# A vision-tower layer on one core: limits exchanged a step earlier, output weights split in two places, factors and residual biases moved into attention steps

## The reference

```python
def reference(x, ...):
    h = s4d_kernel(...)                      # (16, 128, 1024): 16 tiles of 128 tokens, 1024 features
    h = h + attn(layernorm(h), Wq, bq, Wk, bk, Wv, bv, Wo, bo)
    h = h + ffn(layernorm(h), gate, up, down)
    return h

def attn(x, ...):                            # 32 heads of 32 features
    q, k, v = (x @ W.T + b, split into heads)
    scores = where(causal, q @ k.T / sqrt(32), -inf)
    return (softmax(scores) @ v) @ Wo.T + bo

def qlinear(x, q, scale, A, Bm):             # gate, up: 1024 -> 2752, down: 2752 -> 1024
    w = (q - 7.5) * (scale * 0.005)
    return x @ w.T + 0.02 * (x @ A @ Bm)     # A, Bm of rank 32
# ffn(x) = qlinear_down(silu(qlinear_gate(x)) * qlinear_up(x))
```

## Time and profile before

| what | value |
|---|---|
| median of 3 runs | 2070.15 us (2068.34 to 2071.24) |
| the profiled execution: its time, its span | 2068.1 us, 2066.1 us |
| busy in the span: PE, DVE, ACT, POOL | 1894.4, 1166.4, 614.9, 614.3 us |
| attention steps 24 to 31 | 721.3 to 884.4 us of the span |
| output stage | 884.4 to about 1105 us |
| feed-forward stage | about 1105 us to the end |

### The profile page before, as it was taken

How to read it: one execution, slowest core, us unless ns; L and a number is a source line. 1 busy time by engine, 2 the same in 40 slices (tenths; PEclk the granted TensorE clock), 3 DMA queues, 4 the chain that set the end, 5 groups by cost and what they waited for, 6 DMA issues and landing times.

```text
span 2066.1 us, 31321 instructions
## 1 busy us (share of the span) xinstructions
PE 1894.4 (92%) x13212; PEld 1027.5 (50%) x13212; DVE 1166.4 (56%) x1476; ACT 614.9 (30%) x871; POOL 614.3 (30%) x261
## 2 busy tenths in 40 slices
PE   0377699999999988989999999999999999999999
PEld 0377565666666655544554444444444444444444
DVE  8999568777788777755564544444444444211111
ACT  2155333433443334421113333333333233200000
POOL 2675023343343333434211232222223222111101
PEclk9998799999999999999999999999999999999999
DMA  2022212111112111234433232232232132533441
GB/s 90 10 72 61 55 32 55 39 40 36 49 54 66 67 47 52 71 134 150 168 122 98 83 102 79 75 102 90 64 102 92 62 102 78 192 132 109 141 143 42
DMA packets 99812, 173.32 MB, mean 84 GB/s; under 512 B 13984, under 2 KB 75168, under 8 KB 91744
## 3 DMA queue, kind: packets, MB, share of 16 engines
q1 hardware_dynamic: 99680, 171.41, 26.0%
HBM read 114.22 MB, written 56.11 MB: 82 GB/s over the span
## 4 chain that ended last, share of the span: by engine, by line
PE 76%; DVE 6%; POOL 2%; issue 1%; ACT 1%; DMA 1%; SPq 0%; ACTq 0%; DVEq 0%; POOLq 0%
PE acc L1133 15%; PE acc L1207 14%; PE acc L1134 14%; PE ps_p L937 4%; PE ps_p L939 4%; PE ps_p L938 4%; PE ps_t L964 2%; PE acc L1051 2%; PE ps_p L953 2%; PE ps_p L955 2%; PE ps_p L954 2%; PE acc L1052 2%; PE acc L1053 2%; PE ps_l L1149 2%; PE ps_i L1163 1%
## 5 line engine op out<-in xcount | busy, mean ns | idle before, releaser
L1133 PE MATMUL acc<-x_hi,q_f 128*128 128x512 f16 x1376 | 522.0, 379 | 0.0
L1134 PE MATMUL acc<-x_lo,q_f 128*128 128x512 f16 x1376 | 521.5, 379 | 0.0
L1207 PE MATMUL acc<-down_levels,hid_parts 128*128 128x512 f16 x1376 | 300.1, 379 | 0.0
L897 POOL TENSOR_TENSOR prob<-prob,mx 128x1024 f32<-128x1024 f32 x64 | 121.5, 1898 | 405.0 <-DVE mx L1489 405.0
L1133 PEld LDWEIGHTS acc<-x_hi,q_f 128*128 128x128 f16 x1376 | 134.5, 98 | 174.8 <-issue 17.8
L1207 PEld LDWEIGHTS acc<-down_levels,hid_parts 128*128 128x128 f16 x1376 | 133.2, 98 | 163.1 <-issue 5.0
L1134 PEld LDWEIGHTS acc<-x_lo,q_f 128*128 128x128 f16 x1376 | 134.7, 98 | 156.9
L906 POOL TENSOR_SCALAR q_f<-q_raw 128x2048 f16<-128x2048 int32 x22 | 118.1, 5366 | 312.6 <-PE acc L1134 311.8
L937 PE MATMUL ps_p<-x_hi,w_qk 128*128 128x512 f16 x512 | 197.2, 385 | 0.0
L939 PE MATMUL ps_p<-x_hi,w_qk 128*128 128x512 f16 x512 | 196.3, 383 | 0.0
L938 PE MATMUL ps_p<-x_lo,w_qk 128*128 128x512 f16 x512 | 196.3, 383 | 0.0
(11 more groups left out here) (285 smaller groups left out, 3087.1 us busy)
## 6 DMA issues: line engine op xcount, KB each, us to landing
q_raw<-in_gu_q SPq DMA_DIRECT2D x22, 1024.0 KB, 7.2
...
w_raw<-in_w_qk SPq DMA_DIRECT2D x8, 1024.0 KB, 5.2
...
wv_raw<-in_w_o SPq DMA_DIRECT2D x8, 1024.0 KB, 4.9
```

The lines of the kernel that those rows point to most:

```text
L897: nc.gpsimd.tensor_tensor(prob[s % 2][p][:], prob[s % 2][p][:], bc(mx[p][:], H, 2), ALU.subtract).then_inc(s_sub[p], 1)
L1133: nc.tensor.matmul(acc[u % 2][:, m, :], lev, x2_hi[:, k, tok], start=(k == 0), stop=False)
L1134: last = nc.tensor.matmul(acc[u % 2][:, m, :], lev, x2_lo[:, k, tok], start=False, stop=(k == KT - 1))
L1207: last = nc.tensor.matmul(acc[n % 2][:, b, :], parts[n % 3][:, at], levels[:, i, b * CH:(b + 1) * CH], start=(i == 0 and part == 0), stop= ...
```

## The change

- SP exchanges the limits at the head of step 23 instead of its end, and then loads gu_a_raw at once instead of in step 30.
- `WO_STEP` goes from 26 to 25, and the two blocks of Wo of a step are split: the first stands on ACT and DVE before and behind the second part of the probabilities (a = 1), the second before the values. `factors` moves to step 24 of DVE, the Sqrt that feeds it to the head of step 24 of ACT, gu_a's high half to step 25 of ACT and its low half to step 26 of DVE.
- POOL adds the bias to the first two residuals inside the last attention step: one before its subtractions, one between them and its multiplications.
- SP loads the attention output n + 3 before it stores h1 n.

Computation and instruction counts stay the same.

```diff
--- before.py
+++ after.py
@@ -562,7 +562,7 @@
 
 STAT_STEPS = (16, 17, 18, 19, 21, 22)
 LIMIT_STEP = 23
-WO_STEP = 26
+WO_STEP = 25
 
 
 def layer(nc, t, out, first, rooms, small, xn_hi, xn_lo, ident, mask, h0_dram):
@@ -771,6 +771,9 @@
                 sp.wait_ge(s_proj, place(V_STEPS - 1, 2) + 1)
                 for n in range(3):
                     load_output(n)
+            if s == LIMIT_STEP:
+                exchange_limits()
+                sp.dma_start(araw[:], t["gu_a"]).then_inc(s_araw, 16)
             if s >= 2:
                 store(s - 2)
             if c == 0 and j + 1 < KT:
@@ -783,15 +786,12 @@
                 first.exchange(sp, 2 + s // 10)
             if s + 1 in STAT_STEPS:
                 load_job(STAT_STEPS.index(s + 1))
-            if s == LIMIT_STEP:
-                exchange_limits()
             if 0 <= s - WO_STEP + 1 < 4:
                 load_output_weights(s - WO_STEP + 1)
             if s == STEPS - 2:
                 sp.wait_ge(s_wlo, 2 * KT)
                 load_residual(0)
                 load_residual(1)
-                sp.dma_start(araw[:], t["gu_a"]).then_inc(s_araw, 16)
 
         def store_h1(n):
             sp.wait_ge(s_h1, n + 1)
@@ -818,11 +818,11 @@
         sp.dma_start(b_raw[:], t["gu_b"][:, 0, :]).then_inc(s_braw, 16)
         sp.dma_start(ad_raw[:], t["down_a"]).then_inc(s_adraw, 16)
         for n in range(C):
+            if n + 3 < C:
+                load_output(n + 3)
             store_h1(n)
             if n + 2 < C:
                 load_residual(n + 2)
-            if n + 3 < C:
-                load_output(n + 3)
             if n == 2:
                 sp.wait_ge(s_q, 1)
                 sp.dma_start(qraw[:], t["gu_q"][1, :, :, :]).then_inc(s_qraw, 16)
@@ -891,10 +891,19 @@
 
     @block.gpsimd
     def _(pool):
+        def residual(n):
+            pool.wait_ge(s_h0[n % 2], 16 * (n // 2 + 1))
+            nc.gpsimd.tensor_tensor(res[n % 2][:], res[n % 2][:], bob[:], ALU.add).then_inc(s_res, 1)
+
         for s in range(STEPS):
+            if s == STEPS - 1:
+                pool.wait_ge(s_bob, 16)
+                residual(0)
             for p in two:
                 pool.wait_ge(s_max[p], s + 1)
                 nc.gpsimd.tensor_tensor(prob[s % 2][p][:], prob[s % 2][p][:], bc(mx[p][:], H, 2), ALU.subtract).then_inc(s_sub[p], 1)
+            if s == STEPS - 1:
+                residual(1)
             for p in two:
                 pool.wait_ge(s_rc[p], s + 1)
                 nc.gpsimd.tensor_tensor(prob[s % 2][p][:], prob[s % 2][p][:], bc(sm[p][:], H, 2), ALU.mult).then_inc(s_prob[p], 1)
@@ -905,10 +914,8 @@
                 pool.wait_ge(s_mu, (i - 1) * NCH)
             nc.gpsimd.tensor_scalar(q16[i % 2][:], qraw[:], Q_ZERO, None, ALU.subtract).then_inc(s_q, 1)
 
-        pool.wait_ge(s_bob, 16)
-        for n in range(C):
-            pool.wait_ge(s_h0[n % 2], 16 * (n // 2 + 1))
-            nc.gpsimd.tensor_tensor(res[n % 2][:], res[n % 2][:], bob[:], ALU.add).then_inc(s_res, 1)
+        for n in range(2, C):
+            residual(n)
             if n in (2, 6):
                 convert((n - 2) // 4)
         pool.wait_ge(s_acc, C)
@@ -1277,11 +1284,10 @@
             act.wait_ge(s_job, 32)
             nc.scalar.activation(raw_v[0:2 * R, 0:D], raw_v[0:2 * R, 0:D], ACT.Square, accum_out=stat[0:2 * R, 0:1]).then_inc(s_square, 1)
 
-        def high_output_weights(g):
+        def high_output_weights(g, k):
             act.wait_ge(s_wraw, 16 * (g + 1))
             act.wait_ge(s_val, 3 * VPAIRS)
-            for k in two:
-                nc.scalar.activation(woh[:, 2 * g + k, :], raw_v[:, k * D:(k + 1) * D], ACT.Copy, scale=wo_scale[:, g:g + 1]).then_inc(s_woh, 1)
+            nc.scalar.activation(woh[:, 2 * g + k, :], raw_v[:, k * D:(k + 1) * D], ACT.Copy, scale=wo_scale[:, g:g + 1]).then_inc(s_woh, 1)
 
         high_values(0, 0, 0)
         high_weights(0, 0)
@@ -1290,6 +1296,9 @@
         high_values(2, 0, 2)
         for s in range(STEPS):
             j, c, mixed = s // NCH, s % NCH, s <= V_STEPS
+            if s == LIMIT_STEP + 1:
+                act.wait_ge(s_wscale, 1)
+                nc.scalar.activation(a_norm[:], lim[:, 0:1], ACT.Sqrt).then_inc(s_norm, 1)
             if s >= 2:
                 high_prob(s - 2, 3 if mixed else 1)
             if s >= 1:
@@ -1309,9 +1318,13 @@
                 high_prob(s - 1, 0)
             if not mixed:
                 high_output(s - 2)
+            if 0 <= s - WO_STEP < 4:
+                high_output_weights(s - WO_STEP, 0)
             if with_values(s):
                 if s >= 1:
                     high_prob(s - 1, 1)
+                if 0 <= s - WO_STEP < 4:
+                    high_output_weights(s - WO_STEP, 1)
                 high_values(place(s, 2), (s + V_LEAD) // VPAIRS, (s + V_LEAD) % VPAIRS)
                 if s >= 1:
                     high_prob(s - 1, 2)
@@ -1326,11 +1339,10 @@
                 first.high(nc, act, 3, s - 13)
             if s == STAT_STEPS[0]:
                 squares()
-            if s == LIMIT_STEP + 1:
-                act.wait_ge(s_wscale, 1)
-                nc.scalar.activation(a_norm[:], lim[:, 0:1], ACT.Sqrt).then_inc(s_norm, 1)
-            if 0 <= s - WO_STEP < 4:
-                high_output_weights(s - WO_STEP)
+            if s == LIMIT_STEP + 2:
+                act.wait_ge(s_araw, 16)
+                act.wait_ge(s_ups, 1)
+                nc.scalar.activation(ast[:, 0, :, :], araw[:], ACT.Copy, scale=ups[:, 0:1]).then_inc(s_ahi, 1)
         high_prob(STEPS - 2, 1)
         high_prob(STEPS - 2, 2)
         high_prob(STEPS - 2, 3)
@@ -1368,10 +1380,6 @@
                 high_low(VPAIRS - 2)
             high_features(n - 1)
             deviation(n)
-            if n == 2:
-                act.wait_ge(s_araw, 16)
-                act.wait_ge(s_ups, 1)
-                nc.scalar.activation(ast[:, 0, :, :], araw[:], ACT.Copy, scale=ups[:, 0:1]).then_inc(s_ahi, 1)
             if n == 5:
                 high_b(0)
             if n == 9:
@@ -1526,11 +1534,21 @@
             chain.mark(ts(wo_back[:], wo_low[:], 1.0 / W_TOP, None, ALU.mult))
             ts(wo_scale[:], first.back_v[:], wo_top[:], None, ALU.mult).then_inc(s_wscale, 1)
 
-        def low_output_weights(g):
-            for k in two:
-                dve.wait_ge(s_woh, 2 * g + k + 1)
-                stt(wol[:, 2 * g + k, :], raw_v[:, k * D:(k + 1) * D], wo_scale[:, g:g + 1], woh[:, 2 * g + k, :],
-                    ALU.mult, ALU.subtract).then_inc(s_wol, 1)
+        def low_output_weights(g, k):
+            dve.wait_ge(s_woh, 2 * g + k + 1)
+            stt(wol[:, 2 * g + k, :], raw_v[:, k * D:(k + 1) * D], wo_scale[:, g:g + 1], woh[:, 2 * g + k, :],
+                ALU.mult, ALU.subtract).then_inc(s_wol, 1)
+
+        def factors():
+
+            dve.wait_ge(s_norm, 1)
+            chain.mark(nc.vector.tensor_copy(pows[:, 0:1], a_norm[:]))
+            chain.mark(nc.vector.tensor_copy(pows[:, 1:3], lim[:, 1:3]))
+            chain.after(nc.vector.tensor_copy(pows[:, 3:4], lim[:, 5:6]))
+            power_of_two(chain, pows[:], ups[:], W_TOP)
+            chain.mark(ts(ups[:, 0:1], ups[:, 0:1], 2.0 ** 9 / W_TOP, None, ALU.mult))
+            chain.after(ts(b_back[:], pows[:, 1:3], pows[:, 0:1], None, ALU.mult))
+            nc.vector.tensor_copy(down_back[:], pows[:, 3:4]).then_inc(s_ups, 1)
 
         chain.mark(nc.vector.memset(stat[:], 0.0))
         chain.after(nc.vector.memset(eps[:], EPS))
@@ -1575,6 +1593,8 @@
                 low_weights(j + 1, c - 2)
             if with_values(s) and s >= 1:
                 low_prob(s - 1, 1)
+            if 0 <= s - WO_STEP < 4:
+                low_output_weights(s - WO_STEP, 0)
             if more and c == 0:
                 find_big(j + 1)
             if s in (1, 6, 12):
@@ -1591,8 +1611,14 @@
                 statistics(STAT_STEPS.index(s))
             if s == LIMIT_STEP:
                 output_scales()
+            if s == LIMIT_STEP + 1:
+                factors()
+            if s == LIMIT_STEP + 3:
+                dve.wait_ge(s_ahi, 1)
+                stt(ast[:, 1, :, :].rearrange("p k r -> p (k r)"), araw[:].rearrange("p k r -> p (k r)"), ups[:, 0:1],
+                    ast[:, 0, :, :].rearrange("p k r -> p (k r)"), ALU.mult, ALU.subtract).then_inc(s_alo, 1)
             if 0 <= s - WO_STEP < 4:
-                low_output_weights(s - WO_STEP)
+                low_output_weights(s - WO_STEP, 1)
             if with_values(s):
                 low_values(place(s, 2), (s + V_LEAD) // VPAIRS, (s + V_LEAD) % VPAIRS)
                 if s >= 1:
@@ -1633,17 +1659,6 @@
-        def factors():
...
-            nc.vector.tensor_copy(down_back[:], pows[:, 3:4]).then_inc(s_ups, 1)
...
@@ -1686,12 +1701,6 @@
             low_features(n - 1)
             add_residual(n)
             normalise(n)
-            if n == 2:
-                factors()
-            if n == 3:
-                dve.wait_ge(s_ahi, 1)
```

(2 more changed lines are left out.)

7 lines of the change are left out of this document (removed).

## The result

The kernel after takes 2042.11 us (median of 4 runs, 2039.54 to 2046.03), the kernel before, run beside it, 2069.24 us (4 runs, 2067.16 to 2071.24). The ratio is 0.9869 with a 95% interval of 0.9857 to 0.9881: 27 us or 1.3% faster. The prediction was 2042.0 us. The profiled execution took 2039.54 us with a span of 2037.7.

A forecast was written before the change was run, and what follows sets the result against it. PE bounds the kernel behind 960 us, so only steps 24 to 31 and the output stage's start can give: -18.3 - 1.8 - 2.2 - 5.9 = -28.2 us from 2068.1, 2039.9, median 2042.0; range 2037.5 to 2048.

The forecast's parts named there:

- Exchange of the limits: Attention step 24: an earlier exchange removes DVE's wait at output_scales, 29.0 to 21.0 us, -8.0.
- x: Offset of DVE's first mask into an attention step: extra DVE work in the step before minus 1.25, at least 0.72 us.
- The formula: Attention steps: length = 18.49 + x us, the time from DVE's first mask to the next step being fixed.
- Factors: Ten DVE instructions (1.6 us) in step 24 behind w_big lengthen step 25 from 19.6 to 21.2 us, +1.6.
- Output weights: DVE's 4.49 us wait for ACT goes: step 26 +0.4, step 27 (with gu_a's low half) -3.9, step 28 -3.5.
- steps 29 and 30 together -4.9: Step 29 loses the same 3.5 us as step 28; step 30, without a weight step before it, falls 15.6 to 14.2.
- rival 4: Raw output weights arrive late and ACT holds PE in four steps; 2082 us at a 23 us load; chance 0.03.
- The rival taken from the Trainium skill: Steps 24 to 29: many small PE waits make the clock swing, 0.5 to 1.5 us a step, 2045 to 2051; chance 0.11.
- The argument that the chain hides a low clock: Attention steps: 18.49 held through step 27, said to begin with the clock low, so most clock loss is hidden.
- the constant: Attention steps: 18.49 us from DVE's first mask to the next step's start, in calm and disturbed steps alike.
- Residual biases and order of loads: Output stage: DVE's first add no longer waits for its residual, -1.8; an attention output load comes earlier, -2.2 us.
- gu_a: Output stage: PE's 3.04 us wait and the 2.9 us lost to the low clock behind it go, -5.9; lower bound -3.0.

The follow-up runs named there:

- e1: Changed kernel with the limits exchange and gu_a_raw load back at the end of SP's step 23: 2047.12 us, ratio 0.9902 to the kernel before.
- e2: Changed kernel with the exchange behind the store of step 23 but still ahead of its weight load: 2037.52 us (1 run).
- e3: Changed kernel with the output weights made at the end of the step again, still in steps 25 to 28: 2054.62 us, ratio 0.9945 to before.
- e5: Changed kernel with the first two residual biases back behind the attention steps on POOL: 2041.67 us (1 run).
- e6: Changed kernel with the old order in the output stage, h1 store and residual load ahead of the attention output load: 2040.40 us (1 run).
- the second execution: The changed kernel run once more with nothing changed: 2039.99 us, ratio 0.9859 to the kernel before.
- e4: Changed kernel with factors and both halves of gu_a back in the output stage: 2045.60 us, ratio 0.9894 to the kernel before.
- e11: Changed kernel with factors and gu_a back in the output stage and POOL's first gate-weight conversion ahead of the third residual: 2043.22 us (1 run).
- e10: Changed kernel with w_big in DVE's gap, factors and gu_a behind tile 1's normalisation, POOL's first conversion ahead of the third residual: 2028.81 us, ratio 0.9817 to before.

## Why the prediction was right

**Exchange of the limits.** Predicted -8.0, x = 2.53; measured -8.01 and x = 2.50. e1 takes it back alone (7.9), and e2 shows that the cause is the weight load in front, which made the issue late and the write long (5.1 us with it, 1.4 to 2.1 without). The shorter write was not foreseen; the prediction took the old 8.63 us from issue to data as they were and had cover enough. The formula alone would have given 7.3 (28.29 - 21.0): the 8.0 came out because the measured 29.00 was taken, and the 0.7 between them, at a granted clock of 0.88, went with the wait (e1, with the wait back, shows 0.88 in its step 24 again).

**Factors.** +1.6 predicted, +1.53 measured in step 25. The Sqrt and the two table loads cost nothing, as taken.

**Output weights.** +0.4, -3.9, -3.5 predicted; +0.38, -3.94, -3.54 measured. The term that was mis-sized is "steps 29 and 30 together -4.9": it was -5.39, the excess all in step 29 (18.19 to 14.21, -3.98). The saving of 3.5 had been carried over from step 28. In e3 the first mask of step 29 is as late as before (4.63 us in, 4.64 before), and yet the step takes 17.50 us, not 18.19. Step 29 of the kernel before, and of e3:

```profile
836.42:854.61 18.19, 14.98 (x161) 7.13 (x153) 14.45 (x18) 8.22 (x11) 7.55 (x4) 0.91 0.21 73
```

```profile
834.33:851.83 17.50, 13.56 (x160) 6.71 (x153) 14.33 (x17) 7.20 (x9) 7.55 (x4) 1.00 0.06 16
```

In both, PE had waited 2.10 us just before; in the one the granted clock then fell to 0.50, the level of 1.2 GHz, from about 842 to 845 us, in the other it stayed at 1.00. ACT's kh started 15.88 us into the step against 15.18, ahead of the output weights of that step (16.94), so these are not the reason. So 0.69 us of the old step was the clock, a term that the prediction put at nothing in the steps, and 3.29 the chain. That is a little less than the mask's 3.55 (4.64 to 1.09), since steps without values do not come under 14.2: 14.21, 14.19 and 14.23 us with masks at 1.09, 0.12 and 0.96. For them 18.49 + x does not hold at all. ACT nowhere waits for raw weights in these steps, so rival 4 was far away.

**The clock.** The rival taken from the Trainium skill, "TensorE: Matmul & The Clock Gate", section "A second HAM failure mode: psum-queue depth-cycling", did not come about: the granted clock is 1.00 in every window from 720 to 840 us, with idle pieces of 0.2 to 0.9 us in every step. That section describes a kernel in which brief idle times between groups of matmuls make the clock swing; this trace doesn't show it. The argument that the chain hides a low clock held in steps 27 and 28 before, which took 18.50 us beyond their masks, but not in two others: step 29, and step 24, which took 0.7 us more than the constant gives (there no run sets the clock apart). And step 27 did not begin with the clock low, as was said: the clock was 1.00 up to its long wait and 0.57 behind it, from 794 to 798 us.

**Residual biases and order of loads.** Predicted -1.8 and -2.2, -4.0 in all. The transposes of tile 0 come 1.84 us earlier in the stage (33.77 to 31.93), and from them to those of tile 1 it is 2.44 less (13.73 to 11.29); 0.42 is lost again at h_nrm, so up to the transposes of tile 2 3.86 us went (55.04 to 51.18). Taken back singly the two cost 1.83 (e5) and 2.27 (e6). The size of the second was a guess between 1.2 and 2.3 and is at the upper end or just above.

**gu_a.** Predicted -5.9. From the transposes of tile 2 to those of tile 3 it was 18.78 us before and is 12.86 after: -5.92, the wait and the low clock behind it. The reason given for why nothing takes its place, "ACT and DVE reach it earlier by what factors and gu_a took of them", was wrong in one point: h_nrm of tile 2 did get later, and its wait rose from 1.33 us to 1.75 (1.87 in the second execution). It had not been seen that POOL, by moving ahead, would run q_f just when DVE makes h_nrm. That cost 0.42 us. The trace of before already held such a meeting, in a place where PE waits for nothing. The small pass in the row below ends 0.03 us after q_f (970.96 + 5.37 = 976.33); a wider one of the same tile (128x44) takes 0.19 us in the kernel after, where no POOL instruction runs:

```profile
971.39 4.97 DVE L1665 TENSOR_SCALAR gu_scale<-gu_scale,g_hid_up 128x22 f32<-128x22 f32 x1
```

**The sum.** The terms give -28.2, the spans differ by 28.4. The steps gave 0.7 more than predicted, most of it in step 29; the output stage gave 0.1 less, and the execution was 0.3 longer ahead of step 24. So the close sum is in part misses that cancel. That the median came out 0.1 from the forecast is chance: two medians of this kernel differ by 2 us.

Where e4 is set against after, moving `factors` and gu_a is worth not 5.9 - 2.2 = 3.7 us but 7.6, since their old place had become worse through the rest of the change. With POOL out of the way (e11 against e10, from the transposes of tile 2 to those of tile 3, 17.56 against 12.85) it is 4.7 us there: 3.03 of waiting and 1.7 of clock.
